# Where the weight-quantising jobs run beside the second chunk: three per QKV slab and two per attention batch, instead of two and three

## What is computed

```
x = x + layernorm(attn(layernorm(x)))          # attention over the 16 heads of one token
x = x + layernorm(ffn(layernorm(x)))
attn:  qkv = x @ W_qkv (2048 -> 3*2048), scores = q k^T / sqrt(128) within a token,
       softmax, times v, @ W_out + b_out
ffn:   quantize(w) = clip(round(w / (mean|w| + 1e-8)), -1, 1)
       (sigmoid(x @ quantize(w1).T) * (x @ quantize(w2).T)) @ quantize(w3).T
       w1, w2: 5632 x 2048, w3: 2048 x 5632, all float32
```

## Time and profile before

| | us |
|---|---|
| median of 2 runs | 4917.74 (4917.44 to 4918.04) |
| the profiled execution, its time | 4917.79 |
| its span, core 5 (the slowest; cores 4884.7 to 4916.2) | 4916.2 |
| chunk 1, QKV | 391.2 |
| chunk 1, attention | 366.8 |
| chunk 1, output product | 177.5 |
| chunk 1, drain of the quant jobs left | 191 |
| chunk 1, layer norm with residual, to the first feed-forward matmul | 93 |
| the two feed-forward parts and their ends | 2382 |

### The profile page before, as it was taken

One profiled execution on the slowest core, in us unless ns is written; L12 is line 12 of the kernel. 1 busy time (PEld: TensorE's weight loads), 2 busy tenths in 40 slices (PEclk: granted clock), 3 DMA queues, 4 the chain that ended last, 5 costly groups with the idle time before them and its releaser, 6 DMA issues.

```text
span 4916.2 us, 46823 instructions; the slowest of 8 cores (4884.7 to 4916.2 us)
## 1 busy us (share of the span) xinstructions
PE 3263.9 (66%) x15948; PEld 1560.4 (32%) x15948; DVE 1503.1 (31%) x2623; ACT 1063.2 (22%) x1173; POOL 716.2 (15%) x1037
## 2 busy tenths in 40 slices
PE   2777611462499844473237888878976787887993
PEld 1333211220244433332113333333432333333441
DVE  3111122215666799855740000000022000000004
ACT  1666656431155522200000000000000000000000
POOL 1111111220144444433400000000000000000000
PEclk9989855676699955596568999989987898998996
DMA  7888744685388866669632122126443212212445
GB/s 141 257 258 261 247 162 154 227 284 156 122 261 261 250 211 203 202 198 205 190 107 69 52 53 68 52 60 115 94 126 103 69 52 61 59 52 68 93 88 154
DMA packets 734760, 718.41 MB, mean 146 GB/s; under 512 B 307776, under 2 KB 619200, under 8 KB 732352
## 3 DMA queue, kind: packets, MB, share of 16 engines
q0 software_dynamic: 120592, 438.37, 28.7%
q10 hardware_dynamic: 368768, 151.02, 12.8%
q1 hardware_dynamic: 245168, 126.03, 10.4%
HBM read 545.43 MB, written 157.29 MB: 143 GB/s over the span
## 4 chain that ended last, share of the span: by engine, by line
PE 50%; DMA 25%; DVE 13%; issue 7%; ACT 4%; ACTq 1%; SPq 1%; DVEq 0%; POOL 0%; POOLq 0%
PE pbig L1113 21%; PE pbig L1191 9%; DMA wsf<-wqkv 9%; PE pscore L1113 6%; PE pbig L530 4%; PE pbig L716 4%; DMA xstg<-w 3%; DMA wsf<-wout 3%; PE pscore L1191 3%; DVE stats L376 3%; DMA wsf<-w 3%; DMA bandw2b<-qw2T 2%; DMA bandw2a<-qw2T 2%; DVE xcst L950 1%; DVE xcst L955 1%
## 5 line engine op out<-in xcount | busy, mean ns | idle before, releaser
L530 PE MATMUL pbig<-t1f,wsb 128*128 128x512 bf16 x3072 | 718.7, 395 | 131.7 <-DVE wsb L486 128.4
L1191 PE MATMUL pbig<-hid,band 128*128 128x512 bf16 x2112 | 462.6, 381 | 22.9 <-DMA band<-qw3T 22.9
L530 PEld LDWEIGHTS pbig<-t1f,wsb 128*128 128x128 bf16 x3072 | 306.3, 101 | 522.9 <-issue 204.4
L1141 DVE TENSOR_TENSOR hid<-sigst,pbig 128x512 bf16<-128x512 bf16 x88 | 60.5, 688 | 1240.1 <-PE pbig L1113 1240.1
L1113 PE MATMUL pbig<-t1f,bandw1a 128*128 128x512 bf16 x1408 | 311.7, 383 | 167.1 <-DMA bandw1a<-qw1T 167.1
L1124 ACT ACTIVATE sigst<-pbig 128x512 bf16<-128x512 f32 x176 | 105.1, 597 | 1430.9 <-PE pbig L1113 1430.9
L1211 POOL DMA_DIRECT2D yscr<-ttok x64 | 34.6, 541 | 2205.1 <-issue 1650.6
L716 PE MATMUL pbig<-t1f,wsb 128*128 128x512 bf16 x1024 | 272.3, 433 | 95.3 <-DVE wsb L486 91.8
L1113 PE MATMUL pbig<-t1f,bandw1b 128*128 128x512 bf16 x1408 | 307.5, 379 | 0.0
L1113 PE MATMUL pbig<-t1f,bandw2a 128*128 128x512 bf16 x704 | 206.1, 459 | 138.0 <-DMA bandw2a<-qw2T 138.0
L1113 PE MATMUL pbig<-t1f,bandw2b 128*128 128x512 bf16 x704 | 203.7, 454 | 138.4 <-DMA bandw2b<-qw2T 138.4
(11 more groups left out here) (100 smaller groups left out, 4039.6 us busy)
## 6 DMA issues: line engine op xcount, KB each, us to landing
xstg<-w POOLq DMA_DIRECT2D x231, 512.0 KB, 6.0
wsf<-w POOLq DMA_DIRECT2D x128, 512.0 KB, 5.9
ttf<-w POOLq DMA_DIRECT2D x102, 512.0 KB, 8.4
wsf<-wqkv SPq DMA_DIRECT2D x192, 256.0 KB, 7.0
band<-qw3T ACTq DMA_DIRECT2D x128, 352.0 KB, 5.9
xcF<-w POOLq DMA_DIRECT2D x51, 512.0 KB, 8.6
wqkvb<-wsb POOLq DMA_DIRECT2D x48, 512.0 KB, 6.8
wsb<-wqkvb SPq DMA_DIRECT2D x48, 512.0 KB, 5.9
```

Source lines behind the costliest of these rows:

```text
L530: nc.tensor.matmul(p, w, r, start=st, stop=sp),
L1141: nc.vector.tensor_mul(d, a, p), inc="sV")
L1191: nc.tensor.matmul(p, w, r, start=st, stop=sp),
```

## The change

Two numbers are exchanged, in chunk 1 only. Each of the 48 QKV slabs is followed by three quant jobs instead of two, and each of the 32 attention batches by two instead of three. The number of jobs that the stages hold goes from 96, 96, 32 and 48 (QKV, attention, output product, drain) to 144, 64, 32 and 32.

```diff
@@ -543,7 +543,7 @@
         if chunk == 0:
             _gamma_step(b, ctx, 2)
         else:
-            _quant_step(b, ctx, 2)
+            _quant_step(b, ctx, 3)
     for f in range(KD):
         b.consumed(("t1f", f), last_mm)
     mark = ("sS", b.pc["sS"])
@@ -671,7 +671,7 @@
     if chunk == 0:
         _gamma_step(b, ctx, 3)
     else:
-        _quant_step(b, ctx, 3)
+        _quant_step(b, ctx, 2)
     if bt == NB - 1:
         b.consumed("qg", ctx["_attn_lastsc"])
         b.consumed("kg", ctx["_attn_lastsc"])
```

## The result

The changed kernel is slightly slower: the ratio to the kernel before is 1.009 (95% interval 1.0065 to 1.0116), so about 44 us more than 4918 (32 to 57 by the interval). The prediction was 4970 us, a ratio of 1.011. The profiled execution took 4948.45 us, with a span of 4946.9 us on core 3 (cores 4928.3 to 4946.9).

A forecast was written before the change was run, and what follows sets the result against it. TensorE was taken to bound QKV, VectorE the attention, with VectorE waiting for loads in the drain. QKV +196, attention -90, output product +1 and drain -55 sum to +52 us: 4970 us, 8-in-10 range 4905 to 5020.

The forecast's parts named there:

- What bounds each stage: Before the change: QKV bound by TensorE with DMA close behind, attention by VectorE; in the drain VectorE waits for loads.
- QKV, the third job waits for a compare that stands behind a copy: QKV: third transposes wait about 2.7 us for their compare, 4.04 us to the next matmuls; stage +196 us.
- The clock: QKV: TensorE's idle time costs clock, 0.94 us a slab taken from the output product; granted clock at 0.9.
- rival 1: QKV: the clock holds, a slab takes 11.29 us, stage +151, kernel 4925 us; chance 0.18.
- Late loads: QKV: most loads are in time and some are not; today's 0.35 us a slab is kept.
- Attention, -90 us: Attention: 32 fewer jobs, priced at VectorE's 2.72 us a full and 1.66 a half-wide one; bounds -80 to -97.
- Output product, +1 us: Output product: five half-wide jobs instead of six, each worth about 1 us; order unchanged.
- Drain, -55 us: Drain: 16 fewer jobs at 3.42 us each, taken off its fast part; bounds -40 to -64.
- rival 2: QKV: every slab pays the full clock loss, 13.39 us a slab, stage +252, kernel 5026 us; chance 0.15.
- rival 3: QKV: the third job hides like the second, 8.60 us a slab, stage +22, kernel 4796 us; chance 0.04.
- rival 4: QKV: the DMAs set the pace at 262 GB/s, 11.0 us a slab, stage +137, kernel 4911 us; chance 0.05.

The follow-up runs named there:

- e1: Kernel before with three jobs behind each QKV slab and still three behind each attention batch; QKV 589.7 us, attention 361.8 us, 4957.87 us in all.
- e2: Kernel before with two jobs behind each attention batch and still two behind each QKV slab; QKV 391.1 us, attention 271.4 us, 4936.80 us in all.
- e7: Kernel before with each job's load issued in front of the store; QKV 378.9 us, drain 172.8 us, ratio about 0.995.
- e3: Changed kernel without two of three compare instructions of every third QKV job (wrong weights); QKV 557.0 us, wait 1.14 us where loads were in time.
- e4: Changed kernel without loading QKV's weight slabs of chunk 1 from the third on (wrong results); QKV 586.2 us.
- e5: Changed kernel with ten extra unread matmuls in front of the third transposes of each QKV slab; QKV 565.1 us, 4998.33 us in all.
- e6: Changed kernel with each job's load issued in front of the store; QKV 574.8 us, drain 134.3 us, 4945.11 us in all.
- e12: Changed kernel with shortened third compares in QKV (wrong weights), loads in front of stores and four store slots instead of two; QKV 505 us.

## Why the prediction was right

- *What bounds each stage.* Right for TensorE in QKV and VectorE in the attention; e1 and e2 show the stages to be independent. In the drain before, VectorE does wait for loads, as was read (42.9 of 191 us on core 5, and 15.5 for stores), but issuing them earlier won 15 us at most (e7), so what makes them late there is open.
- *QKV, the third job waits for a compare that stands behind a copy.* Right in mechanism and size. The wait of L992 for L961 is 2.62 us (2.7 forecast), the gap 4.11 us (4.04), and 133 to 140 us a core in all. e3 removed compare time and the wait fell by as much; e4 removed DMA traffic and it stayed.
- *The clock.* 0.94 us a slab was forecast from the output product of the earlier trace rows. Most slabs alternate between 6.91 and 8.60 us, 0.85 on average, at 0.92 (0.9 forecast). The rule of the Trainium skill (TensorE: Matmul & The Clock Gate, HAM oscillation) that was weighed against it did not hold here: waits of 2.62 us cost clock in about every second slab. e5 shows that the idle time is the cause. But that the size came out as forecast is in part luck. The output product was read on one core, the slowest, and the cores differ there. On six cores of the kernel before, matmul groups of 8.1 and 8.6 us come back again and again, and the granted clock is 0.91 or 0.92 from 2075 to 2225 us. On cores 2 and 4 it is 1.00 in that window, every group after the first keeps 6.91 us or less, behind the same waits, and the stage takes 162.7 us on core 4 and 177 on core 5 (from its first L716 to its last). The timeline and the window of the stage on core 4:

```profile
2152.94 0.61 PE L992 MATMUL ptb<-identS,xstq 128*128 128x128 bf16 x8 [2.68 <-DVE xstq L961]
2153.39 7.07 PE L716 MATMUL pbig<-t1f,wsb 128*128 128x512 bf16 x31
2160.29 0.61 PE L992 MATMUL pta<-identS,wsfq 128*128 128x128 bf16 x8
2163.59 0.61 PE L992 MATMUL ptb<-identS,wsfq 128*128 128x128 bf16 x8 [2.68 <-DVE wsfq L961]
```

```profile
2069.80:2232.50 162.70, 125.75 (x716) 62.83 (x730) 98.22 (x154) 0.00 (x0) 61.58 (x79) 0.99 0.70 211
```

  Read on that core, the term would have been nearly nothing, and the forecast that of rival 1, 4925 us. In QKV after, no core escapes: the loss is 0.7 to 1.0 us a slab on each. Why a wait of this length costs clock on one core and not on another in the one stage, and on all of them in the other, no run here shows.

- *Late loads.* 0.35 us a slab forecast. What is left after 11.87 us (the mean of 11.02 and 12.71, both starting from the matmuls of a slab) is 589 - 570 = 19 us, 0.40 a slab. The reason was right, too: they are late as they are issued behind a store, which e6 shows (without it VectorE waits for no load in QKV), and not for their bytes, as e4 cut the DMA share to 0.64 and the loads landed no earlier.
- *Attention, -90 us.* Too small by 10; the term that was mis-sized is the stalls. I took the busy time of VectorE off and kept most of the stage's other time. The longest waits of VectorE in the attention, core 4, before (within 1700 to 2060 us) and after (1902 to 2165):

```profile
DVE xcst L950 <- DMA xstg<-w: 10.1, 5, 3.7
DVE xcst L950 <- DMA wsf<-w: 2.9, 5, 1.1
```

```profile
DVE ttok L1001 <- PE pta L992: 1.9, 5, 0.4
DVE wtb L649 <- PE ptb L644: 0.6, 1, 0.6
```

  The 13 us of waits for loads of the kernel before are gone; over the 8 cores they were 9.5 to 15 us and are 0 to 6. That a slot has longer to be filled with two jobs a batch is argued. A batch repeats every 8.35 us, as forecast, from one L950 to the next (core 3):

```profile
2033.70 0.74 DVE L950 TENSOR_SCALAR xcst<-xstg,hgam 128x1024 bf16<-128x1024 f32 x1
2042.05 0.75 DVE L950 TENSOR_SCALAR xcst<-wsf,hgam 128x1024 bf16<-128x1024 f32 x1
```

- *Output product, +1 us.* It came out at -2.6. The two cannot be told apart: cores of the kernel before range from 162.7 to 179.9, by whether their slabs lose clock.
- *Drain, -55 us.* -58.7, 3.67 us a job taken away. Right, though the drains of e3 to e5, with the same 32 jobs and 134.4 us on average, put it at -53. But "the transposing loads stay beside the first 12 or so jobs" overstated them: they hold the core 30 us with no job (e1).
- *The rivals.* The clock did not hold (rival 1); every second slab paid and not every one (rival 2); the third job did not hide (rival 3); the DMA rate did not bind (rival 4, by e4). The Trainium skill's 358 GB/s a core (DMA: Bandwidth & Descriptors, Bandwidth) was not reached by any run in this stage; the highest was 279 over 470 us (e12), and 289 in the best 100 us of one core.
- *The sum.* +52 forecast, +34 in the stages, +41 in the mean span, +44 by the ratio. The 18 us between 52 and 34 are the attention (10) and two terms within the scatter of the stages, the output product and the drain (4 each).

## What to carry to other kernels

Work that is emitted in small jobs between large ones is hidden only up to the depth of its look-ahead: here one job was compared ahead, so two a slab cost only their 0.45 us of TensorE each, and a third brought the time between the slabs' matmuls from 0.9 to 4.1 us. Before moving work to the engine that looks idle, write out the order on each queue and find the first instruction that waits for one emitted behind the gap. When such a limit is removed, look for the next in the waits (here the load behind a store, then the store slots, then probably the DMAs): three edits were needed for what one was expected to give. A price that hangs on the clock is to be read on every core, as one core can show a loss that its neighbour does not have. And price the stage that work is taken from by its whole time, as its stalls may go too.

## What the runs showed of the hardware

- A wait of TensorE of 2.62 us, once in 11.0 to 12.7 us, cost clock in about every second slab of QKV, on all 8 cores: 6.91 and 8.60 us for the same 32 matmuls. Filling 2.2 us of it with matmuls brought the granted clock from 0.92 to 0.99 (e5). In the output product of the kernel before, waits of 2.68 us cost clock on six cores (0.91 or 0.92 from 2075 to 2225 us) and none on cores 2 and 4 (1.00).
- Taking 18% of the bytes away (0.52 of 2.88 MB a slab, e4) left the landing time of the 512 KB loads at 5.9 us against 6.0: here the bytes of the other transfers did not set it. In e12, at a share of 0.90, loads of this size landed after 6.9 to 7.3 us against 6.0 to 6.2 (medians of core 5).
- The DMAs of one core moved 279 GB/s at a share of 0.90 in e12, with all 8 cores at work, where the highest 100 us of the earlier trace rows had 262.
